# Attention and feed-forward block on one core: K and Q projected together, per-row maxima turned later, two pairs of probability tiles summed on VectorE

## The reference

```python
x = x + attn(layernorm(x)); x = x + ffn(layernorm(x))
# attn, 16 heads of 64, per batch
xn = norm(x) * gamma;  q, k, v = xn @ Wq, xn @ Wkv          # 256 -> 1024 each
q = rotary(q) / 8;     k = rotary(k) @ W_bilinear[head]
out = softmax(q @ k.T) @ v;  attn = out @ Wo
# ffn: norm, ternary W1 (256 -> 1024), gelu, norm, ternary W2 (1024 -> 256)
```

## Time and profile before

| what | value |
| --- | --- |
| median of 3 runs | 3529.55 us (3527.23 to 3529.97) |
| the profiled execution's own time | 3532.51 us |
| its span | 3530.7 us |
| granted TensorE clock, mean | 0.99 |
| PE busy, share of the span | 97% |
| DVE | 76% |
| ACT | 66% |
| POOL | 74% |

### The profile page before, as it was taken

One profiled execution on the slowest core, in us unless ns is written; L12 is line 12 of the kernel. 1 busy time (PEld: TensorE's weight loads), 2 busy tenths in 40 slices (PEclk: granted clock), 3 DMA queues, 4 the chain that ended last, 5 costly groups with the idle time before them and its releaser, 6 DMA issues. The chain is left out here.

```text
span 3530.7 us, 71278 instructions
## 1 busy us (share of the span) xinstructions
PE 3439.5 (97%) x21154; PEld 2220.5 (63%) x21154; DVE 2691.1 (76%) x4429; ACT 2312.7 (66%) x4412; POOL 2622.0 (74%) x1279
## 2 busy tenths in 40 slices
PE   6999999999999999999999999999999997999999
PEld 4655555555555555555555555556666654888888
DVE  6677777777777767777777777777777777899998
ACT  2666666666677666666666766666766664555555
POOL 2888888888888888888888888888888894222222
PEclk7999999999999999999999999999999998999999
DMA  5223322232223323333332233222322223233332
GB/s 194 75 100 111 101 94 91 98 119 100 96 99 121 100 89 100 114 95 100 100 120 97 95 100 119 100 99 97 118 91 91 73 86 101 89 97 98 98 96 68
DMA packets 255089, 355.75 MB, mean 101 GB/s; under 512 B 40220, under 2 KB 163484, under 8 KB 250268
## 3 DMA queue, kind: packets, MB, share of 16 engines
q1 hardware_dynamic: 245532, 343.29, 29.5%
q10 hardware_dynamic: 9216, 8.39, 0.7%
HBM read 219.49 MB, written 62.12 MB: 80 GB/s over the span
## 5 line engine op out<-in xcount | busy, mean ns | idle before, releaser
L459 POOL TENSOR_TENSOR prob_sum<-prob_sum,prob 128x1024 f32<-128x1024 f32 x762 | 1876.2, 2462 | 300.2 <-ACT prob L538 251.0
L538 ACT ACTIVATE prob<-scores 128x512 f32<-128x512 f32 x2048 | 1073.2, 600 | 394.9 <-PE scores L820 381.2
L742 DVE TENSOR_REDUCE row_max<-max_scores 128x1 f32<-128x512 f32 x1536 | 987.4, 684 | 433.4 <-PE max_scores L866 417.6
L1032 PE MATMUL attn_out<-prob,v 128*64 128x512 f32 x4096 | 935.3, 598 | 0.0
L811 PE MATMUL scores<-q_hi,k_hi 64*128 64x512 f32 x2048 | 777.7, 417 | 11.4 <-ACT scores L509 6.8
L816 PE MATMUL scores<-q_hi,k_lo 64*128 64x512 f32 x2048 | 749.1, 395 | 3.9 <-issue 3.9
L820 PE MATMUL scores<-q_lo,k_hi 64*128 64x512 f32 x2048 | 751.2, 396 | 0.0
L1032 PEld LDWEIGHTS attn_out<-prob,v 128*64 128x64 f32 x4096 | 271.1, 136 | 549.1 <-issue 547.8
L866 PE MATMUL max_scores<-k_hi,q_hi 64*128 64x512 f32 x1536 | 578.3, 430 | 14.8 <-DVE row_max L742 10.7
L509 ACT ACTIVATE scores<-neg_max_seeds 128x512 f32<-128x512 f32 x1024 | 553.4, 603 | 11.8 <-DMA neg_max_seeds<-neg_max_halves 11.8
L811 PEld LDWEIGHTS scores<-q_hi,k_hi 64*128 64x128 f32 x2048 | 377.1, 185 | 282.0 <-issue 158.2
(11 more groups left out here) (148 smaller groups left out, 4890.1 us busy)
## 6 DMA issues: line engine op xcount, KB each, us to landing
rows<-rows SPq DMA_DIRECT2D x512, 128.0 KB, 2.0
neg_max_seeds<-neg_max_halves SPq DMA_DIRECT2D x128, 512.0 KB, 4.0
w_group<-w_parts SPq DMA_DIRECT2D x30, 1536.0 KB, 6.9
attn_normalised<-z_stage SPq DMA_DIRECT2D x128, 256.0 KB, 2.1
v<-attn_normalised SPq DMA_DIRECT2D x64, 512.0 KB, 4.1
sum_inverted_rows<-sums_inverted SPq DMA_DIRECT2D x126, 256.0 KB, 4.8
x_turned_parts<-x_tile_parts SPq DMA_DIRECT2D x49, 256.0 KB, 2.8
xt_batch<-x_turned_parts SPq DMA_DIRECT2D x7, 1792.0 KB, 10.7
```

Of the source, the lines that this page charges most:

```text
L459: nc.gpsimd.tensor_tensor(sums_of(k, half), a, prob[:, n % RING, :, :], ALU.add).then_inc(added, 1)
L538: nc.scalar.activation(prob[:, n % RING, e, :], S[e][n % 2][:, :], ACT.Exp).then_inc(exped[e], 1)
L742: nc.vector.reduce_max(mx[1 - u][:, e, n // 2, n % 2:n % 2 + 1], bank_of(e, jj)[:, :], axis=AX.X)\
L1032: nc.tensor.matmul(O[rows(e), :], V[k // 2 % 2][:, j, col:col + DH], prob[:, n % RING, e, :], start=j == 0, stop=j == 7).then_inc(pv_made[ ...
```

## The change

In words:

- On PE, the Q projection moves from q1 to q0, behind the K projection. q1 has no extra work left. `turn_max` for the second half moves from the end of q3 into the next span's q0, between the two projections; `turn_max` for the first half moves from q1 to q2, behind the V projection. The probability sums go to bank X[1] instead of M, behind both projections. The bilinear multiplication of K is written as two matmuls of 64 columns each instead of one of 128 with zero blocks.
- On DVE, `rotate` for Q moves to q0, right behind that for K. The low part of Q moves from q1 to q3, between the low part of K and `statistics` (it is now made one span earlier). Two new operations, `pair_tiles`, add probability tiles 6 and 7 at the end of q1, and tiles 10 and 11 at the end of q2.
- On POOL, the two additions for each such pair become one, so there are 12 additions a span.
- On ACT, the seeds stand ahead of the copies of V, and `max_row` moves with `turn_max`: into q0 for the second half, into q2 for the first.
- On SP, `max_rows` and `max_seeds` are placed with these; `load_xt` and the loads of weights stand behind them. The gains of the second norm use the memory of the seeds, and so are loaded after the last seeds are read.

The core of the diff:

```diff
+PAIRED = ((6, 7), (10, 11))
+
+
+def summed_by(k, n):
+
+    if n // 8 == 0:
+        return n if n > 1 else 1, k < T - 1 and n in PAIRED[0]
+    return {8: 7, 9: 7, 12: 9, 13: 10, 14: 11, 15: 12}.get(n, 0), n in PAIRED[1]
...
+        def turned_cols(h):
+            return slice(0, P) if h else slice(2 * P, 3 * P)
...
+                if attn:
+                    max_rows(t - 1, 1)
+                if proj:
+                    for c in two:
+                        swap(Q, t, c)
                 if k >= 2:
                     for h in two:
                         store_z(k - 2, t - 2, h)
+                if k >= 1:
+                    sum_columns(t - 1)
+                if attn:
+                    max_seeds(t - 1, 1)
...
+                if k == T - 1:
+                    for e in two:
+                        wait(sp, seeded[e], 8 * t + 4)
+                        at_rest()
+                    sp.dma_start(*gain_load).then_inc(gain_in, 16)
+                if proj and p % 2 and k < T - 6:
+                    if k == -1:
+                        sp.wait_ge(w_out, 16 * GROUPS)
+                    load_w((p // 2 + 2) % (PAIRS // 2), (p // 2) % 2)
...
+                if k < T - 1 and n in (PAIRED[0][0], PAIRED[1][1]):
+                    return
+                b = prob[:, n % RING, :, :]
+                if k < T - 1 and n in (PAIRED[0][1], PAIRED[1][0]):
+                    wait(pool, paired, 2 * t + half + 1)
+                    b = pair_sum[:, :, :]
+                else:
+                    for e in two:
+                        wait(pool, exped[e], 16 * t + n + 1)
                 if j == 1:
                     wait(pool, l_made, 4 * (t - 1) + 4 * half)
                     a = prob[:, (n - 1) % RING, :, :]
                 else:
-                    wait(pool, added, 14 * t + adds_by(n - 1))
+                    order = (1, 2, 3, 4, 5, 6, 7) if k == T - 1 else (1, 2, 3, 4, 5, 7, 9, 10, 12, 13, 14, 15)
+                    wait(pool, added, 12 * t + order.index(n))
                     a = sums_of(k, half)
-                nc.gpsimd.tensor_tensor(sums_of(k, half), a, prob[:, n % RING, :, :], ALU.add).then_inc(added, 1)
+                nc.gpsimd.tensor_tensor(sums_of(k, half), a, b, ALU.add).then_inc(added, 1)
...
+                                done, in_pair = summed_by(k, n - 8) if n >= 8 else summed_by(k - 1, n + 8)
+                                of = t if n >= 8 else t - 1
+                                if in_pair:
+                                    wait(act, paired, 2 * of + (1 if n >= 8 else 2))
+                                else:
+                                    wait(act, added, 12 * of + done)
                                 nc.scalar.activation(prob[:, n % RING, e, :], S[e][n % 2][:, :], ACT.Exp).then_inc(exped[e], 1)
+                    if attn and q < 3:
+                        seed(t, q + 1)
+                    if q == 0 and attn:
+                        max_row(t - 1, 1)
...
+                    if q == 2 and prep:
+                        if has_tile(k):
+                            wait(act, x_turned, t + 3)
+                        max_row(t, 0)
...
+            def pair_tiles(t, h):
+                a, b = PAIRED[h]
+                for e in two:
+                    wait(dve, exped[e], 16 * t + b + 1)
+                wait(dve, added, 12 * t + (6 if h else -4))
+                nc.vector.tensor_tensor(pair_sum[:, :, :], prob[:, a % RING, :, :], prob[:, b % RING, :, :], ALU.add).then_inc(paired, 1)
...
-                            wait(dve, hi_made[Q], t + 2)
-                            nc.vector.tensor_tensor(QL[1 - u][:, :], rot[Q][:, :], QH[1 - u][:, :], ALU.subtract)\
-                                .then_inc(lo_made[Q], 1)
-                        if proj:
                             rotate(t, Q)
                     if q == 0 and k >= 2:
                         norm_z(k - 2, t - 2)
...
+                    if q in (1, 2) and attn and k < T - 1:
+                        pair_tiles(t, q - 1)
...
+                            wait(dve, hi_made[Q], t + 3)
+                            nc.vector.tensor_tensor(QL[u][:, :], rot[Q][:, :], QH[u][:, :], ALU.subtract)\
+                                .then_inc(lo_made[Q], 1)
...
+                    if q == 0:
+                        if proj:
+                            batch = b + (k + 2) // PAIRS - k // PAIRS
+                            if p % 2 == 0 and k > 0:
+                                pe.wait_ge(w_in[p // 2 % 2], 16 * (2 * batch + p // 4))
+                            if p == 0 and k > 0:
+                                pe.wait_ge(xt_in, 16 * batch)
+                                wait(pe, x_stored[1], 64 * batch)
+                            wait(pe, lo_made[K], 2 * (t + 1) + 1)
+                            project(t, K, 0, p, w, order, x_red[1], 16 * (t + 1) + 2)
+                            project(t, K, 1, p, w, order, x_red[1], 16 * (t + 1) + 3)
+                        if attn:
+                            wait(pe, x_red[1], 16 * (t + 1) + (4 if prep else 0))
+                            turn_max(t - 1, 1)
+                        if proj:
+                            project(t, Q, 0, p, w, order, sin_made[K], 2 * pp + 1)
+                            project(t, Q, 1, p, w, order, sin_made[K], 2 * pp + 2)
...
+                            wait(pe, x_red[1], 16 * (t + 1) + 12)
+                            turn_max(t, 0)
...
-                                nc.tensor.matmul((M if c == 0 else X[0])[:, :], WB[:, p, :], rot[K][:, cols(c)],
-                                                 start=True, stop=True).then_inc(kt_made, 1)
-                        if prep:
-                            turn_max(t, 1)
+                                for e in two:
+                                    nc.tensor.matmul((M if c == 0 else X[0])[rows(e), :], WB[:, p, rows(e)], rot[K][:, cols(c)],
+                                                     start=True, stop=True).then_inc(kt_made, 1)
```

More of the change, by code:

```diff
@@ L384, in span @@
                         sp.dma_start(dst, src).then_inc(late_const, 16)
-                if proj:
[L386 to L389, removed]
+                p = (k + 2) % PAIRS
+                if proj and has_tile(k + 1):
+                    wait(sp, x_normed, t + 2)
+                    at_rest()
+                    load_x(t + 1, k + 1, b + (k + 1) // PAIRS - k // PAIRS)
                 if prep:
@@ L391, in span @@
                     max_rows(t, 0)
[L392 to L412, removed]
+                if proj and has_tile(k) and p != PAIRS - 1:
+                    store_x(t, k, b)
@@ L615, in norm_last @@
             def norm_last(h):
-                for e in two:
-                    wait(dve, seeded[e], 8 * (T - 1) + 4)
+                wait(dve, z_made, 2 * (T - 1) + h)
                 wait(dve, l_made, 4 * (T - 1) + 2 * h + 2)
-                nc.vector.reciprocal(seeds[:, 0, h, :], (X[1], M)[h][:, :]).then_inc(last_inv, 1)
+                nc.vector.reciprocal(inv_rows[:, h, :], (X[1], M)[h][:, :]).then_inc(last_inv, 1)
                 dve.wait_ge(last_inv, h + 1)
@@ L870, in turn_max, with project @@
                 wait(pe, negm_made, 2 * (t + 1) + h + 1)
-                nc.tensor.transpose(X[1][:, 0:P], negm[:, :], ident[:, :]).then_inc(nm_turned, 1)
+                nc.tensor.transpose(X[1][:, turned_cols(h)], negm[:, :], ident[:, :]).then_inc(nm_turned, 1)
+            def project(t, x, c, p, w, order, free, count):
+                wait(pe, free, count)
+                base = 2 * P * (1 - x) + P * (p % 2)
+                for m, (xp, wp, kt) in enumerate(order):
+                    last = nc.tensor.matmul((M if c == 0 else X[0])[:, :], w[:, wp, kt, base:base + P], XT[:, xp, kt, cols(c)],
+                                            start=m == 0, stop=m == len(order) - 1)
+                last.then_inc(proj_made[x], 1)
             def sums(k, t):
-                wait(pe, added, 14 * t + 14)
+                wait(pe, added, 12 * t + 12)
                 for h in two:
@@ L988, in span @@
                             last.then_inc(x_turned, 1)
+                    if q == 2 and prep and not proj:
+                        wait(pe, x_red[1], 16 * (t + 1) + 12)
+                        turn_max(t, 0)
                     if k == T - 1 and q == 1:
```

133 lines of the change are left out of this document (48 added, 85 removed).

## The result

The changed kernel takes **3596.03 us** (median of 4 runs, 3594.82 to 3598.27) beside 3529.71 us (4 runs) for the kernel before on the same chip: a ratio of 1.0192, 95% interval 1.0176 to 1.0209. It is slower, by 66 us where I forecast 44, and inside the range of 3511 to 3600, by 4 us. But the sum that led there was wrong in two of its terms.

What follows compares the result with a forecast made beforehand. PE, busy in 97% of the span, was taken as the bound. 53 spans at +1.03 us (+54.6), nine others (+1.5), batch starts -9 and ends -3 gave +44 us on 3529.55, so 3573 us, range 3511 to 3600.

Steps and rivals of the forecast that it cites:

- PE waits for DVE's first reduction at the fourth MAX of q0, 1.06 us: Start of q0: DVE, late from q3's low part of Q and statistics, holds up PE's fourth MAX by 1.06 us.
- The low part of Q waits for POOL's third addition and takes 2.3 to 2.6 us: DVE in q3: the subtraction falls into POOL's third addition and ends 1.03 us after it, taking 2.3 to 2.6 us.
- PE's own work, -0.08 us a pair: PE in all quads: regrouped matmuls sum to -0.08 us a pair, with bounds of -0.3 and +0.15.
- The turn in q2: PE in q2: the added turn of the maxima costs 0.20 us.
- The going back to the projection behind the turn in q0: PE in q0: changing back to the projection after the turn costs 0.10 us (0 to 0.2).
- The pair sums, 0.05 us in q1: DVE's `pair_tiles`: costs 0.05 us in q1, bounds 0 and 2.4; covered by the V projection in q2.
- POOL's relief: POOL gets 2 x 2.45 us back a span, worth nothing by itself because PE doesn't wait for POOL.
- Seven batch starts, -9: Batch starts: ACT's 1.36 us wait for seeds goes, as they now precede the next x load; -9 us in all.
- The ends, -3: Last spans: earlier column sums save 6 us, late gains cost some 3; -3 us in all, between -7 and +4.
- the rivals: Low part of Q ahead of POOL's third addition or hidden, 3515 (22%); more waits, 3616 (10%); parts cancel, 3531 (8%).

Runs made afterwards that it cites:

- Two experiments: Changed kernel plus eight semaphore increments: statistics ahead of K's low part in q3, 3502.08 us; or low part of Q moved to q0 ahead of K's rotary, 3525.71 us.
- the version without that stall: Changed kernel, statistics first and Q's high and low parts ahead of K's in q3: 3490.51 us with the pair sums, 3504.39 us without.
- 207 and 193 increments: Kernel before plus that many semaphore increments nobody waits for, at the head of VectorE's attention program: 3583.46 us with 207, 3538.38 us with 193.
- two increments: Changed kernel plus two semaphore increments nobody waits for, at the head of VectorE's attention program: 3603.25 us.
- the last runs: Changed kernel, statistics first and Q's high and low parts ahead of K's in q3: ratio 0.9892 to the kernel before; the same without pair sums, 0.9934.

## Why the prediction was right, and where it was wrong

The time lies in the range, and 1 us above the 3545 to 3595 that the forecast itself was given. The wait that decides is as predicted; the total is near in part by luck.

- *PE waits for DVE's first reduction at the fourth MAX of q0, 1.06 us.* Right in place, cause and size: 1.13 us in the quad's scores, 1.19 in the row shown. Two experiments took it away in two ways: to 1.57 us, and the time fell by 50.8; to 1.29 us, where PE's new wait for the bank gave half of it back.
- *The low part of Q waits for POOL's third addition and takes 2.3 to 2.6 us.* Right: 2.63. Ahead of K's low part, where it meets the end of the second addition, it takes 1.53. The Trainium skill states in "SBUF — State Buffer", section "Who interferes with whom", that a VectorE instruction with two SBUF inputs contends with a GpSimd instruction that reads SBUF, and that the one that issues later waits for the whole of the other. The trace agrees: in both places the operation ends 1.1 us after the addition that it met (1.07 and 1.09), and POOL's next addition takes 3.23 and 3.24 us for some 2.4.
- *PE's own work, -0.08 us a pair.* Mis-sized: -0.57, outside the bounds of -0.3 and +0.15 that I gave. Of the 0.49 between them 0.30 lie behind q0. The rows that I hadn't looked at are those of q0 before, here in PE's timeline of the kernel before:

```profile
1503.31 1.66 PE L961 MATMUL shared<-xt_batch,w_group 128*128 128x512 f32 x6
1504.80 1.54 PE L961 MATMUL max_scores<-xt_batch,w_group 128*128 128x512 f32 x6
1506.42 1.07 PE L878 MATMUL shared<-prob_sum,ones 128*32 128x512 f32 x8
```

  Twelve projections take 3.11 us there, and 2.86 in q1. The column sums behind them wait in the code for K's first product with the sine, which DVE ends at 1506.29 here, 0.13 us before they start; that is 0.25 us a pair. The changed kernel makes them wait for the turned maxima instead. I took the price of the matmuls from q1 and the time of q0 as given, so that a wait that the change takes away was priced as work. The turn in q2 cost 0.11 and not 0.20. The going back to the projection behind the turn in q0 cost 0.08, near the 0.10 that I had put: Q's twelve matmuls take 2.94 us there (1565.35 to 1568.29 in the changed kernel).
- *The pair sums, 0.05 us in q1.* Right (nothing), and in the changed kernel the whole part is worth nothing clear of noise. But that POOL's relief "is worth nothing by itself" holds only while PE waits in q0: 14 us in the version without that stall.
- *Seven batch starts, -9.* Right: they held 9.6 us over the usual period before and 0.4 after. The other spans lost 5.5 us against before, with ACT waiting for seeds more often.
- *The ends, -3.* The number came (-3.1), but it isn't shown to be the change's. The wait for column sums is gone, and DVE waits 4.83 us for the late gains. Yet the kernel before with 207 and 193 increments, where DVE still waits 5.5 and 6.2 us for column sums, takes 102.8 and 103.2 us in this stretch: it varies by 3 us with the place of the code.
- *The feed-forward, which I didn't name: +42.1 us.* This is the term that was missing, and the largest of all. I had asked which instructions the change adds and what they cost where they stand, and not where it pushes the code behind them. With the pairs 18.5 us under the forecast (28.6 for 47.1), the start's -1.8 (only -0.1 with two increments) and this, the difference of 65.8 comes out. So the total was near the forecast in part because two errors have opposite signs, which is luck; without the halts the changed kernel is at +0.78%, +27 us.
- Of the rivals none came. What the last runs show is that the regrouping can be a gain: with q3 in another order the same change is 1.1% faster than before.

## What to carry to other kernels

When operations move between engines, look at what stands ahead of the next matmul that hangs on that engine, and order it by when its input is ready: here the same change is 1.9% slower or 1.1% faster by the order of three steps in q3 and a few instructions' place. A delayed engine also holds the buffers that it reads, so its idle time behind a moved operation covers it only if nobody waits for those. When a part of the program that wasn't edited gets slower at its loop's back-edge, with waits that nothing releases, shift its code by a few instructions before looking for a cause in the data; and price what moves from the rows of the place that it goes to, where a wait can hide in them.

## What the runs showed of the hardware

- A loop body that lies unluckily costs 5.2 to 5.8 us of halt at each back-edge on VectorE and about 7 us of the kernel's time, with PE's clock at 0.50 for 6.7 us behind it (in the stretch shown). Eight instructions more ahead of it take away 40 us (1.0192 to 1.0078), fourteen fewer 45. Both kernels also pay some 7 to 8 us at the one back-edge of attention, whose body has over 2000 instructions on VectorE (the period there is 52.9 us before and 52.7 after, against 45.1 and 45.7). With 193 increments it is 49.8, so the place counts there too; which engine's code it is was not looked into.
- Semaphore increments aren't free on VectorE: one takes some 0.1 us. With 207 of them the first statistics of attention start at 41.02 us, and at 27.44 in the kernel before:

```profile
41.02 0.43 DVE L636 BATCH_NORM_STATS2 x_stats<-x_tile 128x6 f32<-128x256 f32 x1 [22.37 <-issue]
```

  With 193 they start at 39.68: 1.34 us for fourteen, 0.096 each. 207 by 0.096 are 19.9 us. Of these 13.6 show; the other 6.3 fell into a wait for `x_tile` that the kernel before has at that place. On PE's side only 0.56 us of the 1.34 show.
- The same subtraction on VectorE (128 x 1024, fp32r) took 1.23, 1.53, 2.63 or 2.86 us, by its place among GpSimd's additions.
